# Graph attention on one core: the first x tile projected in two parts, the first score row spread by transposes of a repeated column, a shorter chain to the first factors

## What is computed

```python
seq = (x @ W_seq).reshape(N, H, DH)                  # N=2048, H=16, DH=32
score1 = einsum('nhd,d->hn', seq, a1)                # "a" scores, one row per head
score2 = einsum('nhd,d->hn', seq, a2)                # "b" scores
scores = leaky_relu(score1[:, :, None] + score2[:, None, :], 0.2)
attn = softmax(scores + (1.0 - adj)[None] * -65500.0, axis=-1)
hidden = einsum('hij,jhd->ihd', attn, seq).reshape(N, 512) @ W_out + b_out
out = layernorm(x + elu(hidden))
```

## Time and profile before

| what | value |
|---|---|
| median of the three runs | 549.42 us |
| lowest, highest of them | 545.85, 550.5 us |
| time of the profiled execution | 546.6 us |
| span in its profile | 544.7 us |
| mean granted TensorE clock | 0.98 |
| PE / VectorE / ScalarE busy | 511.0 / 492.1 / 446.8 us |

### The profile page before, as it was taken

How to read it: one execution, slowest core, us unless ns; L and a number is a source line. 1 busy time by engine, 2 the same in 40 slices (tenths; PEclk the granted TensorE clock), 3 DMA queues, 4 the chain that set the end, 5 groups by cost and what they waited for, 6 DMA issues and landing times.

```text
span 544.7 us, 15410 instructions
## 1 busy us (share of the span) xinstructions
PE 511.0 (94%) x6813; PEld 459.1 (84%) x6813; DVE 492.1 (90%) x762; ACT 446.8 (82%) x454; POOL 33.7 (6%) x64
## 2 busy tenths in 40 slices
PE   4999997679999999999999999999999999989993
PEld 3788884679999999999999999999999999734441
DVE  6688787998999989999999999999999879989886
ACT  1868686989998989999999999999997868146663
POOL 5000000000000000000000000000000000024542
PEclk9999999589999999999999999999999999999998
DMA  7998601002202011010220102202012040014443
GB/s 256 421 401 296 248 2 64 22 2 78 79 2 79 20 63 78 2 79 2 79 80 1 80 2 79 78 3 80 2 79 79 1 137 4 2 53 136 140 135 116
DMA packets 13334, 48.56 MB, mean 89 GB/s; under 512 B 1428, under 2 KB 2452, under 8 KB 9300
## 3 DMA queue, kind: packets, MB, share of 16 engines
q1 hardware_dynamic: 13268, 47.59, 24.1%
HBM read 43.25 MB, written 4.33 MB: 87 GB/s over the span
## 4 chain that ended last, share of the span: by engine, by line
PE 70%; ACT 14%; DVE 11%; issue 2%; DMA 1%; SPq 1%; POOLq 0%; POOL 0%; DVEq 0%; ACTq 0%
PE sums L358 31%; PE bank L370 17%; ACT tring L515 9%; PE sums L291 9%; PE sums L420 8%; DVE tring L732 3%; DVE tring L718 2%; DMA Vp<-in_adj_dram 1%; PE bank L301 1%; ACT low L504 1%; PE sums L279 1%; DVE Vp L679 1%; PE bank L410 1%; DVE xp L673 1%; PE sums L334 1%
## 5 line engine op out<-in xcount | busy, mean ns | idle before, releaser
L515 ACT ACTIVATE tring<-abc,ab 128x2048 int8<-128x2048 f32 x157 | 305.5, 2023 | 0.0
L358 PE MATMUL sums<-Vp,tring 128*128 128x132 f16 x4096 | 246.2, 223 | 13.1 <-DVE Vp L679 5.5
L358 PEld LDWEIGHTS sums<-Vp,tring 128*128 128x128 fp8e4 x4096 | 241.4, 99 | 15.9 <-issue 10.2
L732 DVE TENSOR_TENSOR tring<-adj,tring 128x512 uint32<-128x512 uint32 x256 | 166.3, 682 | 9.2 <-ACT tring L515 9.1
L370 PE MATMUL bank<-Vp,adj 128*128 128x132 f16 x2048 | 126.1, 221 | 0.7 <-DVE Vp L679 0.7
L718 DVE TENSOR_SCALAR tring<-abc,ab 128x2048 int8<-128x2048 f32 x99 | 126.5, 1277 | 0.0
L370 PEld LDWEIGHTS bank<-Vp,adj 128*128 128x128 fp8e4 x2048 | 122.1, 96 | 1.3 <-DVE Vp L679 1.1
L291 PE MATMUL sums<-Vp,abc 128*128 128x272 f32 x256 | 63.5, 402 | 0.0
L420 PE MATMUL sums<-abc,Vp 128*128 128x512 f32 x128 | 57.7, 595 | 1.3 <-ACT Vp L546 1.3
L291 PEld LDWEIGHTS sums<-Vp,abc 128*128 128x128 f32 x256 | 48.9, 196 | 9.6
L420 PEld LDWEIGHTS sums<-abc,Vp 128*128 128x128 f32 x128 | 23.1, 190 | 25.4 <-issue 23.6
(11 more groups left out here) (77 smaller groups left out, 314.7 us busy)
## 6 DMA issues: line engine op xcount, KB each, us to landing
Vp<-in_adj_dram SPq DMA_DIRECT2D x16, 1024.0 KB, 8.2
abc<-a_rows SPq DMA_DIRECT2D x15, 1024.0 KB, 4.6
abc<-in_x_dram SPq DMA_DIRECT2D x16, 256.0 KB, 5.9
Vp<-in_x_dram SPq DMA_DIRECT2D x16, 256.0 KB, 2.9
out_dram<-Vp SPq DMA_DIRECT2D x16, 256.0 KB, 2.1
Vp<-in_L_gnn_W_seq_dram SPq DMA_DIRECT2D x4, 256.0 KB, 3.7
abc<-in_L_gnn_W_out_dram SPq DMA_DIRECT2D x1, 1024.0 KB, 5.4
Vp<-in_L_gnn_b_out_dram SPq DMA_DIRECT2D x1, 256.0 KB, 5.8
```

The lines of the kernel that those rows point to most:

```text
L358: mm = pe.matmul(bank[b][:, c * 2 * VW:(c + 1) * 2 * VW], slot(jt)[:, it * P:(it + 1) * P].bitcast(F8), Vp[:, h, jt, :, :], start=(jt == 0 ...
L515: act.activation(slot(jt), row(h), ACT.Sign, bias=ab[:, jt, H + h:H + h + 1], scale=-1.0).then_inc(u_ready, 1)
L732: dve.tensor_tensor(words, adj8[:, jt, :].bitcast(U32), words, ALU.bitwise_and).then_inc(t_ready, 1)
```

## The change

In phase A, `project` takes a range of columns. Tile 0 is projected in two parts: the 256 seq columns (waiting for W_seq alone) before `turn_x(1)`, and the 16 score columns after the whole `project(1)`; `seq_made` rises by two after it. The order on PE becomes: turn_x(0), project(0) seq columns, turn_x(1), turn_x(2), project(1), project(0) score columns, turn_adj(0), turn_x(3), project(2), turn_adj(1), turn_adj(2), and then as before from t = 3. W_seq pieces 0 and 2 are issued from ScalarE's queue, 1 and 3 from SyncE's. The PSUM banks of a tile become neighbours, so that copy_ab and copy_seq are one instruction for both halves; a2 is negated when it is copied, which makes the two score copies one.

Row 0 is spread by transposes whose input is a score column repeated 128 times; turn_a as such is gone. All scores are transposed later in four 128 x 128 transposes, copied once by ScalarE at tile 2 of head 0, stored in one DMA, and each head's row is read back in 16 pieces of 128 floats.

The largest values of tiles 0 to 14 are reduced ahead; two short operations add tile 15. The diagonal matrix is gone (a repeated `mcol` is multiplied with the identity), the exponential of head 0 reads PSUM, the reciprocal and its scaling are replaced by bit operations. The comparison of mask 1 (VectorE) and mask 0 (ScalarE) is done for the first 1536 columns as soon as three quarters of row 0 are there; VectorE does it before copy_ab(15), ScalarE before copy_row0(3). Head 0's values are split 4 and 12 tiles. The factors of heads 1 to 15 move into head 0's tile loop (ScalarE tile 2, VectorE tiles 1 and 2), the "R" operations from tile 0 to tile 3. The values of heads 1 to 3 move from tiles 0, 5, 10 to 3, 7, 11.

```diff
+PARTS = (slice(0, 4), slice(4, NT))
+SOON = 3 * N // 4
-VALUES_AT = ((0, 5, 10),) + ((1,),) * (H - 1)
-HIGH_AT = ((3, 8, 13),) + ((6,),) * (H - 1)
-LOW_AT = ((5, 10, 14),) + ((9,),) * (H - 1)
+VALUES_AT = ((3, 7, 11),) + ((1,),) * (H - 1)
+HIGH_AT = ((5, 9, 13),) + ((6,),) * (H - 1)
+LOW_AT = ((6, 10, 14),) + ((9,),) * (H - 1)
...
-                sp.dma_start(row(h), scratch[h:h + 1, :].partition_broadcast(P)).then_inc(abc_loaded[h % 2], 16)
+                sp.dma_start(row(h).rearrange("p (t n) -> p t n", n=P),
+                             scratch.rearrange("(t c) n -> c t n", t=NT)[h].partition_broadcast(P)).then_inc(abc_loaded[h % 2], 16)
...
             turn_x(0)
-            for t in range(NT - 2):
+            project(0, slice(0, half))
+            turn_x(1)
+            turn_x(2)
+            project(1)
+            project(0, slice(half, WC)).then_inc(seq_made, 2)
+            turn_adj(0)
+            turn_x(3)
+            project(2).then_inc(seq_made, 1)
+            turn_adj(1)
+            turn_adj(2)
+            for t in range(3, NT - 2):
...
+            def spread_row0(c, tiles):
+
                 for t in tiles:
-                    mm = pe.transpose(turned_a[t // 4][0:H, t % 4 * P:(t % 4 + 1) * P], ab[:, t, 0:H], idf)
+                    mm = pe.transpose(row0_bank[c][:, t % 4 * P:(t % 4 + 1) * P], ab[:, t, 0:1].to_broadcast([P, P]), idf)
...
-            pe.wait_ge(diag_ready, 1)
-            pe.matmul(bank[6][:, 0:2 * H], ones[0:2 * H, :], diag[0:2 * H, :], start=True, stop=True).then_inc(mx_spread, 1)
+            pe.wait_ge(mcol_ready, 1)
+            pe.matmul(Mps, mcol[0:2 * H, :].to_broadcast([2 * H, P]), idf[0:2 * H, 0:2 * H], start=True, stop=True).then_inc(mx_spread, 1)
+            pe.wait_ge(adj_ready[1], NT // 2)
+            for g in range(4):
+                mm = pe.transpose(bank[7][:, g * P:(g + 1) * P], ab[:, 4 * g:4 * (g + 1), :].rearrange("p t c -> p (t c)"), idf)
...
+            act.wait_ge(row0_copied, 3)
+            act.wait_ge(ab_copied, 1)
+            slot_free(act, 0, 0)
+            sign(0, 0, slice(0, SOON))
             copy_row0(3)
...
+                    if h == 0 and jt == 2:
+                        split_high(0, PARTS[1])
+                        factors(1, slice(1, H))
+                        act.wait_ge(a_turned, 1)
+                        act.copy(aT, bank[7]).then_inc(a_copied, 1)
...
+                if t == NT - 1:
+
+                    dve.wait_ge(row0_copied, 3)
+                    slot_free(dve, 0, 1)
+                    above_row(0, 1, slice(0, SOON))
                 copy_ab(t)
```

More of the change, by code:

```diff
@@ L28 @@
 TINY = 2.0 ** -100
+EXPONENT = 0x7F800000
 EDGE = 56.0
@@ L280, in turn_x, with project @@
                 mm.then_inc(x_turned, 1)
-            def project(t):
+            def project(t, columns=slice(0, WC)):
                 r = t % 2
@@ L287, in project @@
                 for k in range(KT):
[L288 removed]
+                    if t == 0 and columns.start == 0:
+                        pe.wait_ge(w_loaded[k], 16)
+                    if t == 1:
                         pe.wait_ge(wa_ready, 2 * k + 2)
                     for s in range(2):
[L291 to L293 removed]
+                        mm = pe.matmul(bank[2 + 2 * r + s][:, columns], xT[:, r, k * P:(k + 1) * P], Wx[:, k, s, columns],
+                                       start=(k == 0 and columns.start == 0), stop=(k == KT - 1), skip_group_check=(t == 0))
+                return mm
             def turn_adj(it):
@@ L320, in _ @@
             pe.wait_ge(x_copied, NT - 1)
-            turn_a(range(0, 4))
-            project(NT - 2)
+            pe.wait_ge(ab_copied, 12)
+            spread_row0(0, range(0, 4))
+            project(NT - 2).then_inc(seq_made, 1)
             turn_adj(NT - 2)
             turn_adj(NT - 1)
-            pe.wait_ge(a_copied, 1)
-            turn_a(range(4, 8))
+            pe.wait_ge(row0_copied, 1)
+            spread_row0(1, range(4, 8))
             pe.wait_ge(x_copied, NT)
[L328 to L334, removed]
-            pe.wait_ge(seq_copied, NT - 1)
-            spread_row0(0)
-            turn_a(range(12, 15))
+            spread_row0(2, range(8, 12))
+            project(NT - 1).then_inc(seq_made, 1)
+            pe.wait_ge(row0_copied, 2)
+            pe.wait_ge(ab_copied, NT - 1)
+            spread_row0(3, range(12, 15))
             pe.wait_ge(ab_copied, NT)
-            turn_a(range(15, NT))
-            spread_row0(1)
+            spread_row0(3, range(15, NT))
             pe.wait_ge(mx_ready, 1)
@@ L380, in _ @@
                 for jt in range(NT if h < H - 1 else NT - LAST):
-                    if h == 0 and jt == NT // 2:
+                    if h == 0 and jt == PARTS[1].start:
                         pe.wait_ge(v_ready, 2)
@@ L426, in _ @@
         def _(act):
+            for k in range(0, KT, 2):
+                load_w(act, k)
             def copy_x(t):
@@ L460, in _ @@
                 if t == NT - 2:
-                    copy_a(0)
+                    copy_row0(0)
                 cast_adj(t + 1)
@@ L464, in _, with sign, factors @@
                     copy_adj(t - 1)
-            copy_a(1)
-            copy_a(2)
-            copy_adj(NT - 1)
-            copy_row0(0)
-            copy_a(3)
             copy_row0(1)
             copy_row0(2)
+            copy_adj(NT - 1)
+            def sign(h, jt, columns=slice(0, N)):
+                return act.activation(slot(jt)[:, columns], row(h)[:, columns], ACT.Sign, bias=ab[:, jt, H + h:H + h + 1], scale=-1.0)
+            act.wait_ge(row0_copied, 3)
+            act.wait_ge(ab_copied, 1)
+            slot_free(act, 0, 0)
+            sign(0, 0, slice(0, SOON))
             copy_row0(3)
-            for n, heads in enumerate((slice(0, 1), slice(1, H))):
+            def factors(n, heads):
                 act.wait_ge(e_in, n + 1)
@@ L708, in finish @@
                     dve.tensor_tensor(acc_h, acc_h, part[0], ALU.add).then_inc(fin_step, 1)
-            for q in range(2):
-                values(0, slice(q * NT // 2, (q + 1) * NT // 2))
+            values(0, PARTS[0])
             for h in range(H):
@@ L717, in compare @@
                     slot_free(dve, h, jt)
-                    dve.tensor_scalar(slot(jt), row(h), ab[:, jt, H + h:H + h + 1], -1.0,
-                                      ALU.is_gt, ALU.mult).then_inc(above, 1)
+                    above_row(h, jt, slice(SOON, N) if h == 0 and jt == 1 else slice(0, N)).then_inc(above, 1)
                 for jt in range(NT):
```

157 lines of the change are left out of this document (79 added, 78 removed).

## The result

The changed kernel takes 670.91 us (median of four executions) against 548.57 us, a ratio of 1.2235 with a 95% interval of 1.2191 to 1.2279. Three of its executions took 669.54 to 671.1 us; the fourth was a slow one of 1061.19 us at a granted clock of 1.00, which the ratio leaves out and no trace explains. The forecast was 546.7 us. The profiled execution spans 667.4 us, 122.7 us more than the 544.7 us before.

The account below looks back on a forecast made before the run. PE bounds the kernel once dense from 123.34 us, so only what precedes counts: 1.3 us later at the start, 2.5 and 0.1 earlier after the last projection. 548.0 - 1.3 = 546.7 us, range 542.8 to 551.0.

Parts of the forecast that it names:

- Without price: the late store of the scores, then rows in pieces of 512 bytes: Row loads for later heads: at worst 15 us a row, each hidden; below 22 us a row nothing shows.
- My list of what would prove me wrong: project(3) under 26.8 us, VectorE idle over 1 us in head 0, or more PE waits for masks or rows.
- Section 1: The start, until PE runs without gaps: costs 1.3 us, between a gain of 0.5 and a loss of 4.0.
- the chain behind them: From the end of tile 0's score columns, copies and casts held by seq_made until project(3) starts: 7.2 us.
- project(1) at 3.67 us: Tile 1's projection in the start, taken at 3.67 us, from 15.3 to 18.95 us.
- Rival (b): Start: adj0 unmoved and score columns at 3.67 us cost 4.0 us against 2.6 gained; 549.4 us, chance 0.15.
- Section 3: T (last projection's end) to dense PE, VectorE-bound: first values 2.5 us sooner, at most 0.1 from work to 16th AND.
- the terms listed for mask 3: Head 0: ScalarE has mask 3 at values start + 7.35, VectorE arrives at + 6.9 and waits 0.45 us.
- The lag of PE: PE's dense start behind VectorE's 16th AND: 1.25 us again, 1.0 to 2.3.
- rival (c): Adjacency rounds: PE's clock stays lower beyond the last mask, 0.8 us, with 0.9 of backlog; 548.4 us, chance 0.08.
- (d): First values: row 0 or copy_adj(15) on ScalarE holds the early factors, gain shrinks to 0.5; 548.7 us, chance 0.07.
- the sum of 1.3 us: Whole kernel: 1.3 us later, 2.5 and 0.1 earlier, together 1.3 us earlier.

Follow-up runs that it names:

- r2_before_pieces: The kernel before, with only the DRAM scratch in runs of 128 floats (8 KB apart) and rows read in 16 pieces of 512 bytes: 767.06 us, ratio 1.400.
- r1: The changed kernel, with the scores stored so that each head's row is contiguous in DRAM and loaded whole again: 544.94 us, ratio 0.9947.
- r9: The changed kernel, with the DRAM scratch padded to 33 runs per tile, pieces 16.5 KB apart, and the store in four DMAs: 544.84 us, ratio 0.9959.
- r10: r2_before_pieces with the scratch padded to 17 runs a tile in place of 16, pieces 8.5 KB apart: 547.33 us.
- r3: The changed kernel, with the 15 row loads issued on GpSimd's queue in place of SyncE's: 678.38 us.
- r6: The kernel before, with rows laid out and loaded in four pieces of 2 KB: 548.52 us.
- r7: r1 with the old start: tile 0 projected in one part in the old PE order, W_seq still on two queues: 544.01 us, ratio 0.9928.
- r11: r7 with all four pieces of W_seq on SyncE's queue again: 543.83 us, ratio 0.9938.

## Why the prediction was wrong

**The step that failed** is "Without price: the late store of the scores, then rows in pieces of 512 bytes". Its bound was "at worst 15 us a row", from the W pieces; a row took 18.5 us, and 27.1 in r2_before_pieces. W's pieces of 1 KB lie side by side in DRAM, 256 KB in one stretch, so that load couldn't bound pieces 16 KB apart. Its second half was the larger error: "below 22 us a row nothing shows". I asked who waits for the row. I didn't ask who shares the DMA engines with it. The DMA queue of instructions stands in the page of before, 53 packets, 0.87 MB, and PE fetches 16 KB about every 7.4 us; r1 and r9 show that this one step makes all of the 122 us. My list of what would prove me wrong had PE waiting "for masks or rows"; it waited for neither.

**Section 1** (a loss of 1.3 us forecast). adj0 gained 1.15 us (1.0 forecast); the 16 score columns took 1.8 us in r1_rows_whole (2.0); the chain behind them 7.3 us in both executions (7.2). The term sized wrong was project(1) at 3.67 us: in the changed kernel's profile it took some 5.4 us at the lower clock, behind PE's wait for copy_x(1). project(3) came 2.8 us late there, 0.9 in r1_rows_whole. Rival (b) named the right place but not this cause; the columns' upper bound of 3.67 us didn't come.

**Section 3** held. Values at T+3.85 forecast, T+3.62 and T+3.63 measured. VectorE's work 28.3 us forecast, 28.06 in both. One sum in it was wrong: the terms listed for mask 3 add up to 7.05 us, not 7.35, and those of VectorE to 6.8, so the wait was 0.25 us by them and not 0.45. Measured, VectorE began AND 3 at + 7.48 us (101.22 us) with a wait below 0.1 us. The lag of PE was 120.96 - 119.97 = 1.0 us in r1_rows_whole against 1.25, with the granted clock at 1.00 from 117 us on; rival (c) didn't come, nor did (d): ScalarE had the Sign of 1536 columns and copy_row0(3) behind it by T+1.2.

So with rows that are quick, the sum of 1.3 us was right in sign and mechanism, not in size: the dense part starts 2.38 us sooner in r1_rows_whole, 1.0 later by the start, 2.75 sooner by the first values, 0.3 by VectorE's work and 0.3 by PE's lag. The runs show 0.3 to 0.7%. Had the layout been padded, the time would have been within 1% of the kernel before (0.9959 in r9_padded_stride).

**What stays open.** That the distance makes rows slow is shown by r9 and r10. Why pieces 8 or 16 KB apart are slow and 8.5 or 16.5 KB are not isn't: that they fall on the same part of DRAM is a guess, and it doesn't say why 8 KB is slower than 16. Whether the fetch waits behind the row's packets in a DMA engine or in DRAM wasn't tested. Two things speak for the first: a fetch waits behind quick rows too, and once it starts, its packet nearly always takes the usual 0.9 to 1.5 us. The exceptions are the fetches in the second row of the changed kernel, 3.5 and 1.8 us; why that row and the fifth let one through is open.

## What to carry to other kernels

When a DMA's layout changes, look up the distance of its pieces in DRAM, and pad it off a multiple of 8 or 16 KB. Shown is one case, 128 partitions that all read the same pieces. A transfer that nobody waits for isn't free: long PE programs fetch their instructions through the same engines, so one transfer must be shorter than the instructions that PE has in hand, some 8 us here. A wait called "issue" in the middle of a ready stream of matmuls is the sign of it; look for the instruction queue in the DMA windows.

## What the runs showed of the hardware that was unexpected

- The same 1 MB in 2048 packets of 512 bytes lands in 27.1 us at a distance of 8 KB, 18.5 us at 16 KB, 5.5 us at 8.5 KB and 5.9 us at 16.5 KB. Pieces of 1 KB at 16 KB took 14.0 us, of 2 KB at 32 KB 8.0 us.
- Instruction fetches wait for the end of a row's flight, whether the row is slow or quick: of 30 slow flights (changed kernel and r3) two let one start before their last 1.1 us, of the 13 fetches in flights of r6 none started before the last 1.3 us. In the changed kernel that was so although a row kept the DMA engines busy for only 27.7% by the profile (another one for 64%). Issuing the row from GpSimd made no difference.
- PE stopped 14.7 to 16.5 us after the start of its last fetch (fetches come every 7.4 us) and went on 1.0 to 1.5 us after the next one had landed.
- VectorE and ScalarE, with 716 and 452 instructions, have no wait put down to "issue" from 100 to 560 us of the changed kernel.
- An idle gap of PE of 2.4 us was followed by a lower clock in one execution, one of 2.0 us in the same code by none in another. Behind the same wait of 1.45 us in the last stage the clock fell in r1, r7 and r9 and not in the kernel before and r11, worth 1.7 us.
- f32 matmuls of 16 columns cost 1.8 us for 16 passes, 0.11 us each, as much as transposes of 128 columns.
